# Decay of a delta-rule attention layer as a running product (a scan) on VectorE, in place of sums on TensorE and Exp on ScalarE

## The reference, cut to what matters

```python
g = -jnp.exp(A_log) * jax.nn.softplus(a + dt_bias)
beta = jax.nn.sigmoid(b)
def step(state, inp):
    qt, kt, vt, gt, bt = inp
    state = state * jnp.exp(gt)[..., None, None]
    pred = jnp.einsum('bhk,bhkv->bhv', kt, state)
    delta = (vt - pred) * bt[..., None]
    state = state + kt[..., None] * delta[..., None, :]
    out = jnp.einsum('bhk,bhkv->bhv', qt, state)
    return (state, out)
```

## Time and profile before

| | before |
|---|---|
| median of 3 runs | 3371.46 us |
| profiled execution | 3380.03 us, its span 3378.3 us |
| busy: PE / DVE / ACT / POOL | 2872.0 / 2101.1 / 1591.6 / 809.3 us |
| first mixture-of-experts block, attention, second block | to about 520, 566 to 2825, from 2825 us |
| granted TensorE clock, mean | 0.934 |

### The profile page before, as it was taken

How to read it: one execution, slowest core, us unless ns; L and a number is a source line. 1 busy time by engine, 2 the same in 40 slices (tenths; PEclk the granted TensorE clock), 3 DMA queues, 4 the chain that set the end, 5 groups by cost and what they waited for, 6 DMA issues and landing times. The chain is left out here.

```text
span 3378.3 us, 60751 instructions
## 1 busy us (share of the span) xinstructions
PE 2872.0 (85%) x19470; PEld 2089.7 (62%) x19471; DVE 2101.1 (62%) x4327; ACT 1591.6 (47%) x4884; POOL 809.3 (24%) x991
## 2 busy tenths in 40 slices
PE   2699992567999999999999999999998985399993
PEld 2466662234777777777777777777777674266662
DVE  3122223577898898898898898898886544122222
ACT  0111110455766676766766666666765551011110
POOL 3100004342232332332323323323320101300003
PEclk6899995778999999999999999999999996699996
DMA  5122201124434434434434434434433311122212
GB/s 179 41 93 90 90 24 52 64 92 140 150 105 137 144 94 144 137 106 144 125 113 137 137 109 127 149 110 128 138 118 93 96 56 66 59 67 84 93 58 81
DMA packets 361526, 352.18 MB, mean 104 GB/s; under 512 B 213940, under 2 KB 283956, under 8 KB 361268
## 3 DMA queue, kind: packets, MB, share of 16 engines
q1 hardware_dynamic: 346676, 288.00, 27.9%
q0 software_dynamic: 14592, 60.83, 5.1%
HBM read 205.47 MB, written 143.26 MB: 103 GB/s over the span
## 5 line engine op out<-in xcount | busy, mean ns | idle before, releaser
L478 PE MATMUL f_ps_up<-f_wbuf,f_xgT 128*128 x1248 | 499.4, 544 | 5.3 <-issue 3.3
L573 DVE TENSOR_TENSOR f_h<-f_h,f_ps_up 128x448 f32<-128x448 f32 x156 | 96.9, 621 | 555.1 <-ACT f_h L547 555.1
L547 ACT ACTIVATE f_h<-f_ps_up 128x448 f32<-128x448 f32 x156 | 84.8, 544 | 635.2 <-PE f_ps_up L478 635.2
L478 PEld LDWEIGHTS f_ps_up<-f_wbuf,f_xgT 128*128 128x128 f32 x1248 | 231.4, 192 | 189.2 <-issue 184.5
L1437 DVE SCALAR_TENSOR_TENSOR at_vT<-at_bank,at_taps_v,at_vT 128x510 f32<-128x510 f32 (+2 forms) x384 | 280.9, 745 | 75.2 <-ACT at_vT L1310 66.1
L1437 DVE SCALAR_TENSOR_TENSOR at_qk<-at_bank,at_taps_qk,at_qk 128x510 f32<-128x510 f32 (+2 forms) x384 | 284.6, 744 | 50.0 <-ACT at_qk L1303 40.2
L1096 PE MATMUL at_bank<-xnT,at_w_qk 128*128 128x512 f32 x512 | 250.0, 612 | 10.0 <-DMA at_taps_qk<-_L_attn_conv_weight_dram 8.5
L1121 PE MATMUL at_bank<-at_w_vz,xnT 128*128 128x256 f32 x1024 | 243.2, 380 | 13.2 <-DVE at_vT L1437 13.2
L1718 POOL TENSOR_SCALAR at_osum<-at_osum 128x8 f32<-128x8 f32 x64 | 15.1, 237 | 984.4 <-ACT at_junk L1414 984.4
L500 PE MATMUL f_ps_y<-f_wbuf,f_hT 128*128 x1092 | 248.8, 379 | 1.6 <-DVE f_hT L577 1.6
L1109 PE MATMUL at_bank<-xnT,at_w_vz 128*128 128x512 f32 x512 | 235.7, 604 | 14.7 <-DVE at_qk L1437 10.6
(11 more groups left out here) (220 smaller groups left out, 6155.2 us busy)
## 6 DMA issues: line engine op xcount, KB each, us to landing
f_wbuf<-in_L_ffn_w_dram POOLq DMA_DIRECT2D x48, 896.0 KB, 7.9
pt_kept<-at_pt_made SPq DMA_DIRECT2D x64, 512.0 KB, 2.6
mt_kept<-at_mt_made SPq DMA_DIRECT2D x64, 512.0 KB, 4.6
at_mt<-mt_kept SPq DMA_DIRECT2D x64, 512.0 KB, 3.5
at_pt<-pt_kept SPq DMA_DIRECT2D x64, 512.0 KB, 4.3
qk_kept<-at_qk SPq DMA_DIRECT2D x64, 256.0 KB, 3.2
ks_kept<-at_ks_made SPq DMA_DIRECT2D x64, 256.0 KB, 3.3
at_ks<-ks_kept SPq DMA_DIRECT2D x64, 256.0 KB, 4.6
```

The lines of the kernel that those rows point to most:

```text
L478: last = te.matmul(ps_up[hf][w][:, 0:MH], xgT[b][:, k, :], wbuf[:, bass.ds(off + (w * WSIZE + k * M + hf * MH), MH)], start=(k == 0), stop ...
L573: v.tensor_tensor(part, part, ps_up[hf][1][:, 0:MH], ALU.mult).then_inc(h_ready, 1)
```

## The change

The decay becomes a running product. For a fixed j, D[j, t] along t is 1 at t = j and each next element is the one before it times exp(g[t]). With `diag_b` (b on the diagonal, zero elsewhere) added in at each step, one scan over 8 x 128 elements a partition gives b * D for all 8 matrices; exp(g) of a chunk's first position is set to zero, so nothing runs over from one matrix to the next:

```diff
+                def scan(u):
+
+                    dve.wait_ge(s["steps_loaded"], 16 * (idx(u) + 1))
+                    dve.wait_ge(s["diag_ready"], idx(u) + 1)
+                    at_least(dve, s["mt_ready"], idx(u))
+                    at_least(dve, s["pt_ready"], idx(u))
+                    v_.tensor_tensor_scan(decay[:].rearrange("p n m -> p (n m)"), steps_e[:],
+                                          diag_b[:].rearrange("p n m -> p (n m)"), 0.0, ALU.mult, ALU.add).then_inc(s["decay_ready"], 1)
+                def mix(u, of):
+                    dve.wait_ge(s["decay_ready"], idx(u) + 1)
+                    dve.wait_ge(s["kq_done" if of else "kk_done"], idx(u) + 1)
                     at_least(dve, s["spilled"][1 - two(u)], SPILL * of_two(shift(u, -1)))
+                    both = gen[0 if of else 2][:].rearrange("p (t m) -> p t m", m=P).unsqueeze(2).to_broadcast([P, Q4, HV, P])
+                    v_.tensor_tensor((pt_made if of else mt_made)[:].rearrange("p (t v) m -> p t v m", v=HV), both,
+                                     decay[:].rearrange("p (t v) m -> p t v m", v=HV),
+                                     ALU.mult).then_inc(s["pt_ready" if of else "mt_ready"], 1)
```

`decay_sums`, `decay_exp` (on ACT and on POOL), `spread_decay` and `fix_diag` are gone. POOL makes `diag_b` with one affine_select out of b. The exp(g) rows are made once, ahead of the loop: four transposes, one Exp, one memset and a store to DRAM. SP then loads a unit's row (4 KB) into all 128 partitions (512 KB written) once an iteration:

```diff
+                def load_steps(u):
+                    at_least(sp, s["decay_ready"], idx(u))
+                    if idx(u) == 0:
+                        sp.wait_ge(steps_stored, 16)
+                    row = steps_kept.rearrange("(u n) t -> u (n t)", n=N8)[bass.ds(idx(u), 1), :]
+                    sp.dma_start(steps_e[:], row.to_broadcast([P, N8 * P])).then_inc(s["steps_loaded"], 16)
+                def diag(u):
+                    pool.wait_ge(s["b_ready"], idx(u) + 1)
+                    at_least(pool, s["decay_ready"], idx(u))
+                    apart()
+                    g.affine_select(out=diag_b[:], in_=per_unit("b", u).unsqueeze(2).to_broadcast([P, N8, P]),
+                                    compare_op=ALU.is_equal, fill=0.0, base=0, pattern=[[0, N8], [-1, P]],
+                                    channel_multiplier=1).then_inc(s["diag_ready"], 1)
```

Since b now sits in M, in P and (through one more small multiply at the end of POOL's `scales`) in `ks`, it goes out of `weigh`, which becomes one copy of 512 columns; the scaling of k moves into a step of its own behind the gates:

```diff
                 def weigh(u, ch):
                     act.wait_ge(s["u_psum"], 2 * idx(u) + ch + 1)
-                    for b in range(2):
-                        for v in range(HV):
-                            n, m = 4 * b + 2 * ch + v, 2 * b + v
-                            last = sc.activation(wv[:, n, :], gen[0][:, P * m:P * m + P], ACT.Copy,
-                                                 scale=tab["b"][:, bass.ds(N8 * idx(u) + n, 1)])
-                    last.then_inc(s["w_ready"], 1)
+                    sc.copy(chunk(wv[:], ch), gen[0][:].rearrange("p (b v m) -> p b v m", b=2, v=HV)).then_inc(s["w_ready"], 1)
+                def ks_(u):
+                    act.wait_ge(s["qk_turned"], 2 * idx(u) + 1)
+                    act.wait_ge(s["kscale_ready"], idx(u) + 1)
```

Two copies go from DVE to ACT: the second half of `y_copy` (686 ns) and the two of `inv_n`. The last copies of `blocks` into `w_low` go from DVE to POOL (`low`). `blocks` is cut into 16 pieces over the four iterations instead of 8 halves. `y_turn`, `turns`, `products`, `on_state`, `output` and `add` are cut in halves, each with its own count. The orders are new; the first lines of two of them:

```diff
+PE_ORDER = (("solve", 0), ("inv_x", 32), ("state",), ("inv_n",), ("y_turn", 0), ("proj_qk", 0), ("turn", 1),
...
+DVE_ORDER = (("inv_x", 32), ("blocks", 0), ("blocks", 1), ("conv_qk", 0), ("conv_qk", 1), ("inv_x", 64), ("add", 0),
```

More of the change, by code:

```diff
@@ L796 @@
 }
-COUNTS = (5, 4, 4, 3, 2, 2, 2, 0)
+COUNTS = (3, 2, 2, 2, 2, 2, 1, 0, 2, 1, 1, 0, 2, 1, 1, 0)
 STEPS = sum(COUNTS)
 FIRST, AFTER = -max(STAGE.values()), -min(STAGE.values())
-SP_ORDER = (("blocks_out",), ("load_vz",), ("load_d",), ("load_t",), ("load_c",), ("blocks_in",), ("load_qk",),
-            ("load_wo",), ("spill",))
-PE_ORDER = (("solve", 0), ("inv_x", 32), ("proj_qk", 0), ("state",), ("inv_n",), ("turn", 1), ("on_state",),
-            ("proj_qk", 1), ("inv_x", 64), ("y_turn",), ("solve", 1), ("turn", 0), ("project", 0), ("project", 1),
-            ("proj_v", 2), ("proj_v", 3), ("decay",), ("z", 0), ("products",), ("inv_last",), ("turns",), ("z", 1),
-            ("output",))
```

343 lines of the change are left out of this document (164 added, 179 removed).

## The result

The changed kernel takes 3252.39 us (median of 4 runs, 3236.28 to 3254.69) where the kernel before takes 3372.85 beside it (4 runs, 3368.84 to 3375.71): 0.963 of it, 95% interval 0.961 to 0.966. That is 120 us less, and inside the range of 3160 to 3295; the forecast was 3211, 161 less. The profiled execution took 3254.69 us, its span 3253.0.

What follows compares the result with a forecast made beforehand. TensorE was taken as the bound, busy 30.95 of 32.29 us a steady iteration. Steady -109, fill -33, drain -20 and ahead of the loop +1 give -161 us: 3219 profiled, 3211 median; range 3160 to 3295 us.

Steps and rivals of the forecast that it cites:

- The scan: On VectorE in each steady iteration: takes 2.3 us and is hidden behind TensorE, up to about 5 us.
- My own walk: New instruction lists timed with the trace's durations: second `output` at 27.7 us needs scan and first multiply, ready near 26.5.
- TensorE's work: Steady iteration: falls from 30.95 to 29.23 us, as the decay matmuls' 1.72 us go.
- the 0.3 for hand-offs: Steady iteration: narrow places at `turns` and both halves of `output` add 0.3 us in all.
- The iteration in which blocks begin: Every fourth steady iteration: VectorE waits for the blocks' store, stall 4 to 6 us, costing 1.5 us.
- The fill: First twelve iterations: first four drop from 17.05 to 12 us each (-20), next eight give -13; together -33 us.
- The drain: Closing iterations of 25.9 us: ten of them get 2.0 us shorter each, -20 us.
- The tables: Ahead of the loop: four transposes, an Exp over 512 columns and a memset add 1 us.
- The load: SyncE's added load of the steps, 512 KB, issued early in the iteration: costs nothing.
- `shape`: Eight VectorE instructions: 1.7 us shorter without POOL's triangle product beside them, 2.2 us in every iteration.
- the hand-offs': Rival, chance 0.27: new narrow places and a later blocks' store eat half the gain; steady 31.2 us, kernel 3283 us.
- TensorE's floor: Rival, chance 0.13: all narrow places hold and half-clock stretches go; steady 29.3 us, kernel 3157 us.

Runs made afterwards that it cites:

- e5: e4 with the scan issued twice, the second waiting for the first: 3253.19 us.
- e8: The changed kernel with the order lists of the kernel before, as far as its steps allow: 3383.02 us.
- e12: e8 with two useless matmuls in TensorE's list between proj_v and z, where the decay's two stood: 3384.06 us.
- e11: e4 with two useless matmuls in TensorE's list ahead of the products: 3244.33 us.
- e1: The changed kernel with a semaphore of its own for the store of q and k, which ScalarE's first q, k filter copy awaits alone: 3230.95 us.
- e4: e1 plus the store of the blocks issued one iteration earlier, ahead of the unit's four stores: 3165.05 us.
- e7: The changed kernel with the steps loaded for the first unit alone, the 63 other loads left out: 3248.11 us.
- e6: e4 with GpSimd's triangle product put back ahead of the select, its result overwritten: 3172.47 us.

## Why the prediction was right or wrong

- **The scan** (2.3 forecast): 2283 ns. Right; the length fits two steps an element, and the length is all of the reason that a run shows. The rule of the Trainium skill in "DVE: opcode table, instruction layouts, handler registers and perf-mode slots", § Datapath and trigger behaviour, half throughput, agrees. What I added, that it is hidden up to 5 us, is wrong. I compared sums of engines; e5 shows 1.17 us an iteration lost at 4.6 us. My own walk had the wait in it ("the second `output` needs the scan and the first multiply", 1.2 us of slack) and I didn't hold the two sentences against each other.
- **TensorE's work** (29.23): with the 0.3 for hand-offs that is 29.5, and k2 to k4 are 29.04 us in the mean, of which TensorE idles 0.2. Right. The reason was half of it: the sum comes out only because the new orders fill the waits (e8, e12 against e11). The same sum of busy times, applied to e8, would have foretold a gain of nearly the same size, and e8 has none.
- **The iteration in which blocks begin** (1.5 us above the rest): the failed term of the steady stretch. It is 34.5, 5.5 above k2 to k4, and but for the first the stall is 6.7 to 8.5 us, not 4 to 6. The 8.0 us from issue to go-on were right (8.2), the filters behind the wait too. Two things were wrong. I had the issue 1 us ahead of `solve` 0 again; it comes 1.1 to 3.0 us behind it (0.3 in the first), so `project` waits 2.8 us, not 0.7. And then TensorE runs at half clock, for 2.7 us more in the k1 shown; I had the earlier trace rows with such a stretch and counted it as rare. k2 gave 1.9 us of it back (28.35 against 30.2 forecast): VectorE, busy 31.7 of 34.4 us there before, is busy 26.4. Net: -92 in place of -109.
- **The fill** (-33): -2.5, the step that failed outright. I wrote that the wait for the store of M, ahead of the scaling of k, goes. It went from that line and stayed at another: `conv_qk` has a wait on the same stores, and I had not followed it. e1 shows it by taking it away: 12.5 us an iteration, where I had said 12. The eight behind the four gave 3.7 us in place of 13; with both edits (e4) they give 10.5.
- **The drain** (-20): -32. The full iterations fell from 25.9 to 23.7 as forecast (24). The ten that I counted gave 21.7. I had left out the last ones, in which only parts of a unit are left: two of 20.5 us became 19.0 and 15.3. The remaining 4 lie behind the last `shape`, 2 of them behind the attention.
- **The tables** (+1): +1.4. That is no test: the first mark stands between 636.9 and 641.5 us in the kernels that have the tables, and at 637.1 before.
- **The load** (nothing): e7, nothing in the steady stretch.
- **`shape`** (2.2 us, with the product gone): right, and e6 shows what it depends on.
- **The rivals.** The measured 3252 is nearer to the hand-offs' 3283 than to the forecast's 3211, but not by their mechanism: in k2 to k4 the new narrow places cost 0.2 us, and the steps' load costs nothing. TensorE's floor, 3157 us, is what e4 reaches (3165; 29.18 us an iteration against 29.3, and no stretch at half clock in the 50), by two edits that the change doesn't have.

Against the profiled execution the sum was 36 us too low: 30 from the fill, where e1 gives back 23, and 17 from k1 less what k2 gave back, less 12 from the drain. That the time fell inside the range is in part luck: what the drain and k2 gave beyond the forecast stands against the fill and k1.

## What to carry to other kernels

Work taken from the engine that bounds is worth its time only if the next thing in its list is ready: look at what the removed instructions covered, for here they covered a wait of 1.4 us, and under the old lists taking them away was worth nothing. A wait on a semaphore that counts several stores is a wait for the last of them; search every place that waits on it before writing that a wait goes, and give a store that is needed early a count of its own. Before moving a step in a list that all iterations share, check the iterations in which it isn't the one that hurts.
